# A three-stage decoder layer: running sums through memory in the mixer, TensorE's attention loop written out, GpSimd's order moved

## The chip, the core and the metric
One core of a Trainium2 chip runs the whole kernel. The time is device microseconds (us) of one execution; three runs of the kernel before are shown, and one more execution carries the profile. TensorE (PE) multiplies into eight banks of PSUM, VectorE (DVE) and ScalarE (ACT) work on PSUM and SBUF, GpSimd (POOL) on SBUF alone, SyncE (SP) issues most DMAs.

## The reference
The input x has 32 sequences of 128 tokens with 128 features. Cut to what matters:

```python
# 1. mixer: 4 heads of 64, state 128, the first 32 features of B and C rotated
alpha = exp(A_t * dt_t); gamma = tr * dt; beta = (1 - tr) * dt * alpha
base = b_t * (x_{t-1} * beta + x_t * gamma)
state = state * alpha + rotated(base, theta_t);  y_t = <state, rotated(c_t)>
x = layernorm(x + ((y + D * x_h) * silu(z)) @ w_out.T)
# 2. cross attention: 16 heads of 8 on ctx_1024, masked softmax over 128 keys
x = layernorm(x + softmax(mask(q @ k.T / sqrt(8))) @ v @ Wo + bo)
# 3. 16 experts of 64, top 2 of 4 groups, top 4 experts, and a shared expert
x = layernorm(x + (x + experts(x) + shared(x)))
```

## The kernel before, in words
The sequences go in eight groups of four, b = 0 to 3. There are three stages, each a block of five engine programs written by hand and tied by semaphores; between blocks all engines meet. `pairs` (line 85) and `ahead` (line 95) run the groups two to a loop turn: `pairs` three turns and two groups written out, `ahead` two turns and four groups written out. `left` is how many groups follow.

**Mixer.** The recurrence is computed as a product per sequence: mix(s, t) = G(s, t) times exp(sum of the exponents A*dt from s+1 to t), zero for s > t, and y = w_tok times mix, with w_tok = gamma * x_s + beta * x_(s-1). The exponents' sums are made per sequence: GpSimd multiplies an upper triangle by the exponent of each head, twice, for a high and a low part (`ramps`, lines 728 to 734), TensorE multiplies both by a strict lower triangle (`after`) and adds a mask of -30000 (`acausal`) into one bank, PD (`front`, line 854), and ScalarE takes one exponential of 4 x 128 columns (line 693). The other bank of `front`, PX, holds x of the tokens and of the tokens before them (`tokens`, line 865); VectorE scales its halves by gamma and beta (`inputs_of`, line 785). PG holds G (`scores`). `back` (line 897) makes y in PY0 and PY1, `skip` (line 888) starts them with D * x, once a group; its six products mark where a group begins on TensorE. Beside a group runs the preparation of the next: `theta` (cumulative angles), `angles`, `fractions` (VectorE, lines 383 to 391), `sines`, `features` (B and C, in P0 and P1), `rotate` (VectorE, lines 761 to 770), `gates`. VectorE forms x + output and its statistics, GpSimd normalises (`normalise_pool`, lines 141 to 148). In the last group the attention's first projections are mixed in: `part_third` is GpSimd's part of them, after which SP stores the parts (line 265) and loads them stacked (line 276, eight DMAs for the keys and eight for the queries).

**Attention.** In TensorE's group g (line 1473) run the transposed scores and products of g, the scores of g+1 (VectorE reduces their maxima, line 1237, and splits them in three bf16 parts, `split_maxima`, lines 1248 to 1261; TensorE transposes the parts in `max_rows`, line 1457) and the projections of g+2 from x1, staged by SP in `xs` (line 1029), and from the context. GpSimd per group casts the masks (`masks`), makes the projections' third parts and the context's remainder (`context_lo`), normalises the group before and adds the output bias (`biased`, line 1081). In group 5 it issues the loads of the expert weights, in group 6 it splits them (`split_weights`, lines 1623 to 1626); at the head of group 7 TensorE, VectorE and ScalarE wait for that (`e.steps`, PREPARED).

**Experts.** Not touched.

## Time and profile before

| | us |
|---|---|
| median of 3 runs | 678.86 |
| lowest, highest | 673.94, 679.98 |
| the profiled execution | 679.41 |
| its span, first to last instruction | 677.7 |
| TensorE busy (matmuls) | 600.6, 89% |
| VectorE busy | 498.2, 74% |
| GpSimd busy | 261.2, 39% |
| ScalarE busy | 255.8, 38% |

The mixer's preparation ends at some 46 us, its groups at 249, the attention at 473; the experts take the rest. A matmul's recorded end is modelled and overlaps the next one's start, so what a TensorE instruction takes is read from start to start. "issue" names time in which an engine waited for nothing that the profile shows. The mean granted TensorE clock is 0.96 of full speed.

### The profile page before, as it was taken

Reading aid. Unit: us, or ns where it says so; the run is one execution under the profiler, and the core shown is the slowest. Engines: PE = TensorE matmul, PEld = TensorE weight load, DVE = VectorE, ACT = ScalarE, POOL = GpSimd, SP = SyncE. Lnnn points to the kernel's source line nnn. Section 1 sums busy time; section 2 is a strip of 40 time slices with the busy share of each in tenths; the row PEclk is TensorE's granted clock in tenths of the full one; section 3 lists DMA queues with packets and bytes.
Section 4 is the critical chain, followed back from the end, with each engine's and each line's share of the span. In section 5 each row is a group of like instructions: output and inputs, shape, how many; then the busy total and the mean of one; then the engine's idle time right before and its main releaser. Section 6 shows DMA issues by size and latency. Waiting matters only on the chain. (4 is left out here: it accounts for less than half of the span.)

```text
span 677.7 us, 17999 instructions
## 1 busy us (share of the span) xinstructions
PE 600.6 (89%) x6368; PEld 494.8 (73%) x6368; DVE 498.2 (74%) x1246; ACT 255.8 (38%) x444; POOL 261.2 (39%) x301
## 2 busy tenths in 40 slices
PE   6589999999999855699799999877999999999994
PEld 6467777777787643578678777655888888888884
DVE  3867977977977738368688888656688787887863
ACT  2443533533543320356446655343332232232220
POOL 4264646647645628624244346091110110110111
PEclk9979999999999978699899999899999999999998
DMA  7020000000000067064464555400000000000000
GB/s 211 0 63 1 17 15 0 15 15 0 15 16 1 12 176 219 17 171 138 124 176 117 142 133 154 119 7 2 32 1 32 31 0 32 31 29 2 17 16 16
DMA packets 39186, 39.29 MB, mean 58 GB/s; under 512 B 4609, under 2 KB 30753, under 8 KB 39121
## 3 DMA queue, kind: packets, MB, share of 16 engines
q1 hardware_dynamic: 37200, 35.69, 18.4%
q0 software_dynamic: 704, 1.92, 1.1%
q10 hardware_dynamic: 1216, 0.79, 0.5%
q8 instruction: 44, 0.72, 0.5%
q14 instruction: 22, 0.17, 0.1%
HBM read 24.10 MB, written 10.88 MB: 52 GB/s over the span
## 5 line engine op out<-in xcount | busy, mean ns | idle before, releaser
L1911 PE MATMUL bank<-xT_hl_c,w_up 128*128 128x512 f32 x432 | 119.7, 413 | 2.4 <-ACTq L67 2.4
L141 POOL TENSOR_TENSOR rstd<-mv,norm_c 128x4 f32<-128x4 f32 x24 | 6.4, 268 | 272.0 <-DVE mv L135 257.1
L1237 DVE TENSOR_REDUCE nmax<-bank 128x4 f32<-128x512 f32 x112 | 72.0, 685 | 31.0 <-PE bank L1393 26.7
L1145 ACT ACTIVATE prob<-bank 128x512 f32<-128x512 f32 x128 | 69.4, 594 | 56.1 <-PE bank L1393 46.8
L1911 PEld LDWEIGHTS bank<-xT_hl_c,w_up 128*128 128x128 f32 x432 | 77.2, 192 | 16.2 <-ACTq L67 2.6
L1833 ACT ACTIVATE sg<-bank 128x512 f32<-128x512 f32 x72 | 43.0, 597 | 106.7 <-PE bank L1911 106.7
L1927 PEld LDWEIGHTS bank<-w_down,hid 128*128 128x128 f32 x576 | 74.4, 191 | 5.9 <-issue 0.5
L732 POOL TENSOR_TENSOR ramp<-upto,dec_hl 128x512 fp32r<-128x512 f32 x64 | 66.8, 1072 | 27.2 <-PE bank L860 27.2
L1927 PE MATMUL bank<-w_down,hid 128*128 128x128 f32 x576 | 75.6, 275 | 0.0
L1383 PE MATMUL bank<-neg_i,mask 64*128 64x256 bf16 x512 | 52.7, 286 | 17.9 <-ACT prob L1145 5.8
L1866 DVE TENSOR_TENSOR gu<-sg,bank 128x512 f32<-128x512 f32 x64 | 43.9, 685 | 21.9 <-PE bank L1911 10.0
L1870 DVE TENSOR_TENSOR hid<-gu,bank 128x512 f32<-128x512 f32 x64 | 44.0, 688 | 7.1 <-DVE gu L1866 1.0
L868 PE MATMUL bank<-w_x,xhl 128*128 128x256 f32 x192 | 42.2, 329 | 0.0
L1383 PEld LDWEIGHTS bank<-neg_i,mask 64*128 64x128 bf16 x512 | 16.9, 97 | 33.2 <-issue 11.7
L1437 PE MATMUL bank<-prob,v_d 128*32 128x128 f32 x1024 | 36.4, 286 | 0.0
L1433 PE MATMUL bank<-prob,ones_s 128*32 128x128 f32 x1024 | 34.6, 276 | 0.8 <-ACT prob L1145 0.8
L420 PE MATMUL bank<-xhl,w_feat 128*128 128x512 f32 (+1 forms) x96 | 29.9, 447 | 5.4 <-DVE b_rot L766 4.4
L868 PEld LDWEIGHTS bank<-w_x,xhl 128*128 128x128 f32 x192 | 29.6, 191 | 6.1 <-issue 5.3
L880 PE MATMUL bank<-c_rot,b_rot 128*128 128x256 f32 x128 | 32.8, 378 | 0.0
L1433 PEld LDWEIGHTS bank<-prob,ones_s 128*32 128x32 f32 x1024 | 26.0, 109 | 6.1 <-issue 2.2
L1437 PEld LDWEIGHTS bank<-prob,v_d 128*32 128x32 f32 x1024 | 28.2, 114 | 2.9 <-ACT prob L1145 0.2
L1071 POOL CAST mask<-mask 128x512 bf16<-128x512 uint8 x32 | 19.3, 612 | 27.3 <-PE bank L1393 22.2
(227 smaller groups left out, 1250.1 us busy)
## 6 DMA issues: line engine op xcount, KB each, us to landing
k_stack<-k_scratch SPq DMA_DIRECT2D x32, 128.0 KB, 2.7
q_stack<-q_scratch SPq DMA_DIRECT2D x32, 128.0 KB, 2.9
k_scratch<-k_part SPq DMA_DIRECT2D x16, 192.0 KB, 2.5
q_scratch<-q_part SPq DMA_DIRECT2D x16, 192.0 KB, 2.5
x<-xT_in SPq DMA_DIRECT2D x8, 256.0 KB, 8.4
mask<-mask_in SPq DMA_DIRECT2D x8, 256.0 KB, 4.7
xres<-x_in SPq DMA_DIRECT2D x8, 256.0 KB, 2.9
k_stack<-k_scratch SPq DMA_DIRECT2D x32, 64.0 KB, 3.0
```

Source lines behind the costliest of these rows:

```text
L732: pool.tensor_tensor(ramp[:, b % 2, v, :, :], bc(upto[:, None, :], [P, HEADS, P]), bc(dec_hl[:, v, bass.ds(g * GS + b, 1), :].rearrange("p ...
L868: mm = pe.matmul(PX[:, shift * D_INNER:(shift + 1) * D_INNER], xhl[:, par, a, b, 1 - shift:P + 1 - shift], w_x[:, v, :], start=(n == 0), s ...
L1145: act.activation(prob[:, b % 2, ORDER[n], :, :], (TT0, TT1)[n % 2][:, :], ACT.Exp, scale=XD ** -0.5)\
L1237: dve.tensor_reduce(nmax[:, b, 4 * u:4 * u + 4], (SS0, SS1)[n % 2][:, :].rearrange("p (i k) -> p i k", i=4), AX_X, ALU.max, negate=True).t ...
L1383: pe.matmul(banks[j][:, :].rearrange("p (i h k) -> p i h k", i=4, h=2)[:, :, half, :], mask[rows, par, b, kind + ver, :], bc(neg_i[rows, N ...
L1433: mm = pe.matmul(U1[32 * u:32 * u + 32, 0:P], ones_s[:, 4 * b + i, :, :].rearrange("p r c -> p (r c)"), prob[:, b % 2, u, i, :], start=(b ...
L1437: mm = pe.matmul(U0[32 * u:32 * u + 32, b * P:(b + 1) * P], v_d[:, par, b, i * P + 32 * u:i * P + 32 * u + 32], prob[:, b % 2, u, i, :], s ...
L1833: act.activation(sg[:, k, :], GG[k][:, :], ACT.Silu).then_inc(a_s.sem, 1)
L1866: dve.tensor_tensor(dst, sg[:, k, :], UU[k][:, :], ALU.mult).then_inc(v_gu.sem, 1)
L1870: dve.tensor_tensor(hid[:, c, :], gu[:, k, :], WW[(c - 1) % 2][:, :], ALU.mult).then_inc(v_hid.sem, 1)
L1911: mm = pe.matmul(bank[:, :], w_up[:, which, a, c, :], xT_hl[par][:, v, :], start=(n == 0), stop=(n == 2))
L1927: mm = pe.matmul(PO[:, b * P:(b + 1) * P], hid[:, c, b * P:(b + 1) * P], w_down[:, c, :], start=(c == 0 and b == 0), stop=(c == NC - 1), s ...
```

## The change
Mixer: the sums of the exponents are formed once for half of the sequences at a time, by two products with the upper triangle: one gives them as rows (64 rows of sequence and head, 128 tokens), one as columns. ScalarE copies both out, the columns negated (`upto_s`); SP stores the rows in DRAM and loads each sequence's four rows back to all 128 partitions (`load_row`). GpSimd sets the acausal half to -30000 (`causal`), and ScalarE takes four exponentials, one a head, with the negated column as bias (`expos`), one sequence ahead. Ramps, the strict triangle and PD are gone; PX has two banks in turn. VectorE's operations on the two halves of fractions, rotation and inputs become one each. GpSimd's normalisation waits for the next fraction. Attention: TensorE's eight groups are written out, and it transposes x1 in place (`xs` and its DMA are gone); GpSimd's context remainder and last masks move ahead of the normalisation, which waits for the end of VectorE's split of the maxima.

The pieces are, in order: the sums and rows; fractions; GpSimd's mixer group; rotation; GpSimd's attention group; the end of TensorE's attention.

```diff
+        def sums(pe, half, bank):
+            dec = decay[:, HALVES[half], :].rearrange("p b h -> p (b h)")
+            pe.wait_ge(s_coef, half + 1)
+            pe.matmul(bank[64 * half:64 * half + 64, 0:P], dec, upto[:, :], start=True, stop=True)
+            pe.matmul(bank[:, P:P + 64], upto[:, :], dec, start=True, stop=True).then_inc(s_sums, 1)
+        def load_row(sp, g, b):
+            sp.wait_ge(s_exp.sem, s_exp.at(g - 1, HEADS * b + HEADS - 1))
+            sp.dma_start(rows[:, b, :, :], rows_dram[bass.ds((g * GS + b) * HEADS, HEADS), :]
+                         .rearrange("h t -> (h t)").partition_broadcast(P).rearrange("p (h t) -> p h t", h=HEADS))\
+                .then_inc(s_row[b].sem, 16)
+        def causal(pool, g, b):
+            pool.wait_ge(s_row[b].sem, s_row[b].at(g))
+            pool.affine_select(out=rows[:, b, :, :], in_=rows[:, b, :, :], compare_op=ALU.is_ge, fill=NEG, base=0,
+                               pattern=[[0, HEADS], [1, P]], channel_multiplier=-1).then_inc(s_sel.sem, 1)
+        def expos(act, g, b):
+            act.wait_ge(s_sel.sem, s_sel.at(g, b))
+            act.wait_ge(s_mix.sem, s_mix.at(g, b - 2))
+            for h in range(HEADS):
+                act.activation(expo[:, b % 2, h, :], rows[:, b, h, :], ACT.Exp,
+                               bias=upto_s[:, bass.ds(g * GS + b, 1), h]).then_inc(s_exp.sem, 1)
...
         def fractions(dve, g):
-            for k in range(2):
-                dve.wait_ge(s_ang.sem, s_ang.at(g, k))
-                dve.tensor_scalar(whole[:, k, :], ang[:, k, :], ROUND, -ROUND, ALU.add, ALU.add).then_inc(s_whole.sem, 1)
-            for k in range(2):
...
+            dve.wait_ge(s_ang.sem, s_ang.at(g, 1))
+            dve.tensor_scalar(whole[:, :, :], ang[:, :, :], ROUND, -ROUND, ALU.add, ALU.add).then_inc(s_whole.sem, 2)
+            dve.wait_ge(s_whole.sem, s_whole.at(g, 1))
+            dve.wait_ge(s_trig.sem, s_trig.at(g - 1, 1))
+            dve.tensor_tensor(frac[:, :, :], ang[:, :, :], whole[:, :, :], ALU.subtract).then_inc(s_frac.sem, 2)
...
             def group(g, par, left):
-                ramps(g, (2, 3))
-                if left:
-                    ramps(g + 1, (0, 1))
                 if left == 2:
                     steps_of(pool, g + 2)
                 if left:
+                    for b in range(GS):
+                        causal(pool, g + 1, b)
+                    if left == 2:
+                        pool.wait_ge(s_frac.sem, s_frac.at(g + 2, 1))
                     normalise_pool(pool, g, s_res, s_x1, res, mv, rstd, norm_c, x1[:, bass.ds(g * GS, GS), :])
...
             def rotate(g, par):
-                for k in range(2):
-                    dve.wait_ge(s_trig.sem, s_trig.at(g, k))
-                    dve.tensor_tensor(b_rot[:, par, k, :], P0[:, :], trig[:, k, :], ALU.mult).then_inc(s_prod.sem, 1)
+                dve.wait_ge(s_trig.sem, s_trig.at(g, 1))
+                dve.tensor_tensor(b_rot[:, par, :, :], bc(P0[:, None, :], [P, 2, GT]), trig[:, :, :], ALU.mult).then_inc(s_prod.sem, 2)
                 dve.wait_ge(s_feat.sem, s_feat.at(g, 1))
-                for k in range(2):
-                    dve.tensor_tensor(c_rot[0:64, par, k, 0, :], P1[0:64, :], trig[0:64, k, :], ALU.mult)
-                    dve.tensor_tensor(c_rot[64:P, par, k, 1, :], P1[64:P, :], trig[64:P, k, :], ALU.mult).then_inc(s_prod.sem, 1)
+                for j in range(2):
+                    half = slice(64 * j, 64 * j + 64)
+                    dve.tensor_tensor(c_rot[half, par, :, j, :], bc(P1[half, None, :], [64, 2, GT]), trig[half, :, :], ALU.mult)\
+                        .then_inc(s_prod.sem, 1)
...
-            def group(g, par, left):
-                if left >= 2:
-                    masks(g + 2, par, (2,))
+            def rest(g, par, left):
                 if left >= 3:
                     context_lo(g + 3, 1 - par)
                 if left >= 2:
-                    masks(g + 2, par, (3,))
+                    masks(g + 2, par, (2, 3))
+
+            def group(g, par, left):
                 if left == 2:
                     load_weights(pool, d, e)
                 if left == 1:
                     split_weights(pool, e)
                 if left:
                     head(g + 1, 1 - par, left - 1)
+                    rest(g + 1, 1 - par, left - 1)
+                    if left >= 2:
+                        pool.wait_ge(v_split.sem, v_split.at(g + 2, 7))
                     normalise_pool(pool, g, v_res, g_out, res, mv, rstd, norm_c, x2[:, bass.ds(g * GS, GS), :])
                     biased(g + 1)
...
-            ahead(pe, group)
+            for g in range(NG):
+                group(g, g % 2, NG - 1 - g)
```

On TensorE in the mixer, one sequence of the loop's body before, from `front` on (waits in brackets):

```order
L859 MATMUL bank<-ramp,after 128x512 [waits expo_ready]
L859 MATMUL bank<-ramp,after 128x512
L860 MATMUL bank<-acausal,ident 128x512
L868 MATMUL bank<-w_x,xhl 128x256 [waits w_ready]
L868 MATMUL bank<-w_x,xhl 128x256 x2
L900 MATMUL bank<-mix,w_tok 64x128 [waits w_ready]
L900 MATMUL bank<-mix,w_tok 64x128 x3
L868 MATMUL bank<-w_x,xhl 128x256 x3
L877 MATMUL bank<-plain 128x512 [waits mix_ready]
```

The same in the change:

```order
L912 MATMUL bank<-w_x,xhl 128x256 [waits w_ready]
L912 MATMUL bank<-w_x,xhl 128x256 x5
L943 MATMUL bank<-mix,w_tok 64x128 [waits w_ready]
L943 MATMUL bank<-mix,w_tok 64x128 x3
L920 MATMUL bank<-plain 128x512 [waits mix_ready]
```

Three wide products are gone, and all six token products stand ahead of the back products.

On GpSimd at the end of the attention before, from the last load of the expert weights through group 5's normalisation and bias to the weights' split (max_parts is VectorE's split of the maxima):

```order
L1615 DMA bias<-gate_bias_in 128x16
L141 TENSOR_TENSOR rstd<-mv,norm_c 128x4 [waits x2_sum_ready]
L142 TENSOR_TENSOR res<-res,mv 128x512
L144 TENSOR_TENSOR rstd<-rstd,norm_c 128x4 [waits x2_ready]
L148 TENSOR_TENSOR x<-res,rstd 128x512 [waits x2_ready]
L1081 TENSOR_TENSOR xb<-x,b_o 128x512 [waits x2_sum_ready]
L1623 CAST w_up<-w_raw 128x1152 [waits expert_weights]
```

And in the change:

```order
L1657 DMA bias<-gate_bias_in 128x16
L141 TENSOR_TENSOR rstd<-mv,norm_c 128x4 [waits x2_sum_ready,max_parts]
L142 TENSOR_TENSOR res<-res,mv 128x512
L144 TENSOR_TENSOR rstd<-rstd,norm_c 128x4 [waits x2_ready]
L148 TENSOR_TENSOR x<-res,rstd 128x512 [waits x2_ready]
L1118 TENSOR_TENSOR xb<-x,b_o 128x512 [waits x2_sum_ready]
L1665 CAST w_up<-w_raw 128x1152 [waits expert_weights]
```

The normalisation of group 5 has one wait more, max_parts, and the weights' split is queued behind it.

## Rows read from the trace of the kernel before

**Rows 1.** Busy time by stretch: mixer, attention (us and instructions; granted clock, DMA share, GB/s).
```profile
46.00:222.00 176.00, 170.79 (x1062) 135.78 (x1061) 141.74 (x285) 72.16 (x105) 94.41 (x91) 1.00 0.03 9
276.00:473.00 197.00, 171.96 (x3738) 138.28 (x3737) 145.59 (x334) 99.60 (x189) 82.05 (x93) 0.97 0.40 112
```

**Rows 2.** Timeline of TensorE in one mixer group (start, us, line, xcount, [idle before]).
```profile
110.59 0.62 PE L859 MATMUL bank<-ramp,after 128*128 128x512 f32 x2
111.09 0.70 PE L868 MATMUL bank<-w_x,xhl 128*128 128x256 f32 x3
111.73 0.66 PE L900 MATMUL bank<-mix,w_tok 128*64 128x128 f32 x8
112.32 0.62 PE L868 MATMUL bank<-w_x,xhl 128*128 128x256 f32 x3
112.77 0.86 PE L877 MATMUL bank<-plain 96*128 96x512 f32 x3
114.15 1.76 PE L420 MATMUL bank<-xhl,w_z 128*128 128x512 f32 x6
```

**Rows 3.** Timeline of TensorE: first and last start of the skip product, of eight.
```profile
47.58 1.66 PE L893 MATMUL bank<-xhl,w_dx 128*128 128x512 f32 x6
222.33 1.65 PE L893 MATMUL bank<-xhl,w_dx 128*128 128x512 f32 x6
```

**Rows 4.** Waits in the mixer: who for whom, us in total, times, longest.
```profile
PE bank L859 <- POOL ramp L732: 4.2, 6, 1.0
```

**Rows 5.** VectorE: line 391 of all groups (ns min/median/max); timeline of rounding and rotation.
```profile
L391 DVE TENSOR_TENSOR frac<-ang,whole x16: 676/680/1524, 31.0 to 202.6; 128x512 f32<-128x512 f32 x16
100.28 0.75 DVE L387 TENSOR_SCALAR whole<-ang 128x512 f32<-128x512 f32 x2
104.81 1.28 DVE L766 TENSOR_TENSOR b_rot<-bank,trig 128x512 f32<-128x512 f32 x2
```

**Rows 6.** Timeline of ScalarE: 128 elements, the exponential of 512, a table load.
```profile
17.08 0.31 ACT L552 ACTIVATE e<-soft 128x128 f32<-128x128 f32 x1 [2.13 <-DVE soft L603]
99.75 0.60 ACT L693 ACTIVATE expo<-bank 128x512 f32<-128x512 f32 x1 [1.43 <-PE bank L860]
101.73 1.28 ACT L368 ACT_TABLE_LOAD   x1 [1.38 <-DVE frac L391]
```

**Rows 7.** Timeline of GpSimd: an affine select of 512 elements.
```profile
264.19 0.88 POOL L1120 TENSOR_SCALAR_AFFINE_SELECT ones_s<-ones_s 128x512 f32<-128x512 f32 x1
```

**Rows 8.** DMA issues of the page (KB each, median us to landing).
```profile
xres<-x_in SPq DMA_DIRECT2D x8, 256.0 KB, 2.9
```

**Rows 9.** Timeline of TensorE, GpSimd and SP at the mixer's end.
```profile
232.48 0.72 PE L859 MATMUL bank<-ramp,after 128*128 128x512 f32 x2 [2.92 <-POOL ramp L732]
...
230.39 4.04 POOL L732 TENSOR_TENSOR ramp<-upto,dec_hl 128x512 fp32r<-128x512 f32 x4
...
244.50 4.02 SPq L276 DMA_DIRECT2D q_stack<-q_scratch  x8
```

**Rows 10.** Waits of TensorE in the attention.
```profile
PE bank L1457 <- DVE npart L1261: 6.1, 6, 1.7
```

**Rows 11.** VectorE: line 1257, one of the split's small operations (ns min/median/max).
```profile
L1257 DVE TENSOR_TENSOR nrest<-nmax,npart x16: 192/193/1248, 262.7 to 443.7; 128x32 f32<-128x32 f32 x16
```

**Rows 12.** Timeline of TensorE at the turn of the attention's loop.
```profile
332.34 0.39 PE L1383 MATMUL bank<-neg_i,mask 64*128 64x256 bf16 x4 [2.49 <-issue]
```

**Rows 13.** Timeline of TensorE in a group of straight code.
```profile
421.96 0.39 PE L1383 MATMUL bank<-neg_i,mask 64*128 64x256 bf16 x4 [0.84 <-issue]
```

**Rows 14.** Timeline of TensorE, GpSimd and VectorE around the last attention group.
```profile
432.70 0.61 PE L1383 MATMUL bank<-neg_i,mask 64*128 64x256 bf16 x4 [2.90 <-DMA q_stack<-max_scratch]
452.39 0.66 PE L1735 MATMUL bank<-ident,x 128*128 128x128 f32 x4 [1.10 <-POOL w_up L1626]
...
440.17 0.20 POOL L141 TENSOR_TENSOR rstd<-mv,norm_c 128x4 f32<-128x4 f32 x1 [15.34 <-DVE mv L135]
...
443.29 0.35 DVE L1255 CAST npart<-nmax 128x32 bf16<-128x32 f32 x1
```

More of the change, by code:

```diff
@@ L339, in mixer @@
         s_prod = sem("feat_dve", 8)
-        s_ramp = sem("ramp_ready", 8)
-        s_dec = sem("decay_mm", GS)
+        s_row = [sem(f"row_loaded{b}", 1, 16) for b in range(GS)]
+        s_sel = sem("row_causal", GS)
+        s_sums, s_summed = (ctx.enter_context(nc.semaphore(n)) for n in ("sums_mm", "sums_copied"))
+        s_stored = ctx.enter_context(nc.semaphore("rows_stored"))
+        pool_passed = ctx.enter_context(nc.semaphore("mixer_pool_passed"))
+        rows_dram = nc.dram_tensor("sum_rows_scratch", (NSEQ * HEADS, P), F32, kind="Internal").ap()
+        rows = sb("rows", [P, GS, HEADS, P])
         s_xx = sem("x_mm", GS)
         s_g = sem("g_mm", GS)
-        s_exp = sem("expo_ready", GS)
-        s_w = sem("w_ready", 3 * GS)
+        s_exp = sem("expo_ready", GS * HEADS)
+        s_w = sem("w_ready", 2 * GS)
         s_mix = sem("mix_ready", GS)
@@ L485, in _ @@
                 sp.dma_start(a.cin[:, :, :], d["ctxT"][:, 0:2 * GT].rearrange("p (g t) -> p g t", t=GT)).then_inc(s_att, 16)
+                for b in range(GS):
+                    s_row[b].prime(sp)
+                store_sums(sp, 0)
+                sp.wait_ge(s_stored, 16)
+                for b in range(GS):
+                    load_row(sp, 0, b)
+                store_sums(sp, 1)
                 sp.wait_ge(s_att, 9 * 16)
@@ L489, in _ @@
             def _(pool):
-                for s in (s_ramp, s_turns):
+                for s in (s_sel, s_turns):
                     s.prime(pool)
@@ L533, in _ @@
                 pe.wait_ge(s_pool, 2)
+                sums(pe, 0, PX0)
                 theta(pe, 0)
@@ L536, in _ @@
                 features(pe, 0, 0, (0, 1))
+                sums(pe, 1, PX1)
             @block.scalar
@@ L655, in group @@
                     .then_inc(s_x.sem[par], 16)
+                if left:
+                    for b in range(GS):
+                        load_row(sp, g + 1, b)
                 if not left:
@@ L726, in _ @@
                 s.prime(pool)
-            def ramps(g, bs):
-                for b in bs:
-                    pool.wait_ge(s_dec.sem, s_dec.at(g, b - 2))
-                    for v in range(2):
-                        pool.tensor_tensor(ramp[:, b % 2, v, :, :], bc(upto[:, None, :], [P, HEADS, P]),
-                                           bc(dec_hl[:, v, bass.ds(g * GS + b, 1), :].rearrange("p o h -> p (o h)")[:, :, None],
-                                              [P, HEADS, P]), ALU.mult).then_inc(s_ramp.sem, 1)
             def group(g, par, left):
-                ramps(g, (2, 3))
-                if left:
-                    ramps(g + 1, (0, 1))
                 if left == 2:
@@ L742, in group @@
                 if left:
+                    for b in range(GS):
+                        causal(pool, g + 1, b)
+                    if left == 2:
+                        pool.wait_ge(s_frac.sem, s_frac.at(g + 2, 1))
                     normalise_pool(pool, g, s_res, s_x1, res, mv, rstd, norm_c, x1[:, bass.ds(g * GS, GS), :])
@@ L747, in group @@
                 if left == 1:
-                    pool.memset(a.first[1][:, :, :, :].bitcast(F32), TWO_ONES).then_inc(a.ones, 1)
+                    pool.memset(a.first[1][:, :, :].bitcast(F32), TWO_ONES).then_inc(a.ones, 1)
+            for b in range(2):
+                causal(pool, 0, b)
             coefficients(pool, 1)
-            ramps(0, (0, 1))
             betas(pool, 1)
             steps_of(pool, 1)
+            for b in range(2, GS):
+                causal(pool, 0, b)
             pairs(pool, group)
```

140 lines of the change are left out of this document (66 added, 74 removed).

## The prediction

> **What bounds the kernel now.** I read the stretches of busy time first, then TensorE's own line in each, then its waits, and only then the engines it waits for. In the mixer (46 to 222 us) and in the attention (276 to 473 us) TensorE is the busiest engine, 171 us of 176 and 172 of 197, with VectorE next at 142 and 146 [rows 1]. The busy share alone doesn't say that TensorE is the bound, so look at one sequence of the mixer: its pieces stand back to back [rows 2]. The third stage, the experts, is untouched by the change and keeps its time. The chain of waits on the page covers only that stage, so it says nothing of the two that change, and I leave it.
>
> **The mixer's steady part.** Between the first and the last start of the skip product lie 222.33 - 47.58 = 174.8 us, seven groups [rows 3]. What the change takes from TensorE is, per sequence, the two ramp products and the mask product. Their starts take 111.09 - 110.59 = 0.50 us; the mask product's own run falls under the next record: the three token products behind it take 111.73 - 111.09 = 0.64 us, the same three without it 112.77 - 112.32 = 0.45 us [rows 2]. So 0.50 + 0.19 = 0.69 us a sequence, 28 sequences between the two marks: 19.3 us. TensorE's waits on the ramps between the marks, 4.2 us in all [rows 4], go too.
>
> What comes next late? VectorE's rotation. Before, the sine of the first half could start when the first fraction was done; now one fraction operation covers both halves, the sines wait for it, and one operation waits for both sines. From the end of the first mix: rounding and fraction about 2.0 us (two roundings take 0.75 us, two fractions 2 x 0.68 less the overlap), the table load 1.28 us, two sines of about 0.6 us each, and rotation in three operations of 1,024 elements, about 1.2 us each by the pair at 1.28 [rows 5, 6]: 8.1 us. TensorE meanwhile has back products 0.59, scores 1.38, features 1.6, six token products 0.90, back 0.59, scores 1.38 and half of features 0.8 [rows 2]: 7.2 us, and then wants the rotated C. I therefore charge a new wait of 0.6 us a group (it can be nothing, and 1.5 if VectorE is held up): 7 x 0.6 = 4.2 us back. Nine VectorE operations fewer a group save a start each, under 0.1 us, and a fraction that collides with GpSimd runs up to 1.52 us instead of 0.68 [rows 5]; the normalisation now starts behind it. I take nothing for that by itself: it is what lets VectorE keep pace with a shorter group. Sum: 19.3 + 4.2 - 4.2 = 19.3, taken as **19 us**. Bounds: 10 (VectorE doesn't keep pace: a new wait of 1.9 us a group) and 26 (no new wait, and what TensorE waits for a mix gone too).
>
> What is added is off this path. ScalarE runs four exponentials of 128 elements with a bias for one of 512: by the row of 128 elements 4 x 0.31, and no row has a bias from a tile at this size, so I allow 0.1 for it: 1.2 to 1.6 us against 0.60 [rows 6], four times a group, 4 us on an engine busy 72 us of 176 [rows 1]; each is done one sequence ahead of its mix. Were that cover gone, each sequence would pay 0.6 to 1.0 us. GpSimd's causal select takes 0.88 us by the nearest row of its size [rows 7] in place of two ramps; queued behind it are the next steps and the normalisation, which nobody wants for half a group. SP issues four loads of 256 KB a group; a load of that size lands in 2.9 us [rows 8], and at least a third of a group lies between a row's release and its use.
>
> **The mixer's start.** GpSimd's exponent product now stands ahead of the turns (+0.3 us), the merged fraction delays the first sine (+0.6), and the stage's first block ends only after ScalarE's two copies of the second sums and SP's store (+0.6). Against it, the first group's three products and the wait for the ramps go. Net +0.5, bounds 0 and +2.
>
> **The mixer's end.** In the last group TensorE waits 2.92 us for a ramp, and GpSimd's third part of the keys starts only behind four ramps, at 230.39 + 4.04 = 234.4; SP's sixteen loads of the stacks hang on it, and their last eight are issued until 244.50 + 4.02 = 248.5 us, which ends the stage [rows 9]. Without ramps that part starts when they did, at 230.4, 4.0 us earlier. The store, the landing and the stacks follow at the same distance. **-4.4 us** (the queries' part gains a little more), bounds -2 and -5.
>
> **The attention.** Three edits have a price.
> - Once a group, six times, TensorE waited for VectorE's split of the maxima, 6.1 us in all [rows 10]. Its small operations take 0.19 us, but up to 1.25 when GpSimd's biases and remainders run [rows 11]. GpSimd now waits for the end of that split. Of the 6.1 us I leave out the longest, 1.7, which I place before the last group, where a later wait covers it (below): -4.4 us, taken as -4.5.
> - TensorE's loop is written out. At the turn of the loop it stands 2.49 us with nothing to wait for [rows 12], and its clock then drops for a while; the same product takes 0.61 instead of 0.39 us after such a stop [rows 12, 14]. Half speed over some 3 to 4 us costs about 1.5 more, with a short stop behind it: -4.5 us. In written-out code it once stood 0.84 us for the same reason, while the weights were loading [rows 13]. The Trainium skill ("Runtime: NRT & Kernel Launch", section on instruction fetch mechanics) says that straight code is fetched ahead and mostly hidden; by the page nothing comes back, by that row up to 2.5 us over three new straight groups. I take nothing, and keep 2.5 in the range.
> - GpSimd's new wait stands ahead of group 5's normalisation, and behind it are the bias and the splitting of the expert weights, for which TensorE waits at the last group. Before, that chain began at 440.17 and TensorE went on at 452.39, 12.2 us later, after 1.10 us of waiting. Now it can't begin before the split of the last maxima ends: it starts at 443.29 and takes 4 x 0.19 us and its gaps, 444.1 [rows 11, 14]. TensorE then goes on at 456.3: **+4.0 us**, and as it stands there for 456.3 - (452.39 - 1.10 - 1.7) = 6.7 us, another 1.5 at half speed: +5.5. This is where the change costs.
> The weights' own loads are issued some 4 us later than before; the 2.90 us that TensorE waits for a row of maxima behind them [rows 14] may move either way: 0, bounds -3 and +3. The direct use of x1 instead of a staged copy removes a DMA that nobody waited for: 0. Sum of the attention: -4.5 - 4.5 + 5.5 = **-3.5 us**.
>
> **Total.** 679.4 (the profiled execution, 0.6 us above the runs' median) - 19 - 4.4 + 0.5 - 3.5 = 653.0, so 652.5 in terms of the median. I say 653.
>
> **Rivals.**
> - **VectorE becomes the mixer's bound.** Causal selects read and write SBUF too; if they hold up VectorE's operations on two SBUF tiles as other GpSimd work does (1.52 against 0.68 us [rows 5]), four a group of 0.88 us [rows 7] cost up to 3.5 us a group, and half of it on the path takes 12 us of the 19 back: 665. For it: VectorE is busy 142 of 176 us already. Against: the ramps were 64 such operations of 1.0 us [rows 9] and the path still was TensorE's. The page "SBUF — State Buffer" of the Trainium skill (section on who interferes with whom) gives this as a rule: a VectorE instruction with two SBUF inputs contends with a GpSimd one that reads SBUF, and one waits the other out. Chance 0.2.
> - **Row loads bound the mixer; slower than before.** Each load reads the same 2 KB for all 128 partitions; no row shows a broadcast of this size. Four a group must pass in the time of one group, about 25 us. At 2.9 us each [rows 8] they fit twice over; from 25 / 4 = 6.3 us a load on, the mixer is slower than today, and at 8 us it takes 32 us a group, 7 x 7 = 49 us more, less what the end still gains: 720. Chance 0.04.
> - **More than I count.** No new wait at the rotation, the others gone too, and no wait behind the weights: 26 + 4.4 + 6.5 = 37: 642. Chance 0.12.
> - **The attention loses.** The late chain takes the weights and the wait for maxima with it, stops of instruction fetch appear: +8 us: 661. Chance 0.09.
> My forecast, 647 to 659, gets 0.55.
>
> **Numbers.** About 1% (7 us) is what a measurement of this kernel can tell from no change. The range 642 to 667 holds the forecast, the third rival, the fourth and most of the first. Faster by over 1% (below 672): 0.90; within 1%: 0.05, the worst of the first and the fourth together; slower by over 1%: 0.05.
>
> **What to look at afterwards.** The starts of the skip product should lie 22.3 us apart on average, 25.0 before. The fraction should run in about 1.2 us, never over 2; the small operations of the split at 0.19 us without exception; no stop at the loop's turn; the stage's last stack issue some 23 us earlier than 248.5. In the last attention group TensorE should stand 6 to 7 us for the split weights, with the low clock behind it. I am wrong if TensorE waits for mix or for the rotation by over 1 us a group, if a load of a row takes over 6 us, or if the stop at the weights is short.

## The result

The changed kernel takes 655.6 us (median of 4 runs, 655.1 to 656.8) where the kernel before took 677.8 on the same chip (4 runs, 673.9 to 680.0): ratio 0.9669, 95% interval 0.9635 to 0.9703. The forecast was 653, the range 642 to 667. The profiled execution took 656.8, its span is 655.0. Run again later beside the last experiments it gave 655.8 us, ratio 0.9653 (0.9616 to 0.969).

### The profile page after: what moved, and what is told of

The parts are those of the page before. It is cut to its first block and busy times, and to the rows that moved or that the text cites. A ratio compares the mean times of both kernels' runs of the same rounds, so it can differ in the third digit from the quotient of the medians.

```text
span 655.0 us, 17900 instructions
## 1 busy us (share of the span) xinstructions
PE 582.7 (89%) x6280; PEld 484.8 (74%) x6280; DVE 474.6 (72%) x1174; ACT 277.4 (42%) x544; POOL 208.0 (32%) x260
## 3 DMA queue, kind: packets, MB, share of 16 engines
q1 hardware_dynamic: 41104, 42.57, 22.4%
## 5 line engine op out<-in xcount | busy, mean ns | idle before, releaser
L1953 PE MATMUL bank<-xT_hl_c,w_up 128*128 128x512 f32 x432 | 118.1, 409 | 2.4 <-ACTq L67 2.4
L141 POOL TENSOR_TENSOR rstd<-mv,norm_c 128x4 f32<-128x4 f32 x24 | 4.8, 201 | 299.9 <-DVE mv L135 178.7
L1424 PE MATMUL bank<-neg_i,mask 64*128 64x256 bf16 x512 | 52.8, 286 | 14.1 <-ACT prob L1186 5.7
L477 ACT ACTIVATE expo<-rows,neg_sums 128x128 f32<-128x128 f32 x128 | 40.9, 391 | 13.5 <-DVE mix L858 13.4
L422 PE MATMUL bank<-xhl,w_feat 128*128 128x512 f32 (+1 forms) x96 | 32.2, 461 | 9.0 <-DVE b_rot L817 4.5
L1424 PEld LDWEIGHTS bank<-neg_i,mask 64*128 64x128 bf16 x512 | 16.9, 97 | 29.8 <-ACT prob L1186 11.2
L920 PE MATMUL bank<-plain 96*128 96x512 f32 x96 | 30.8, 429 | 0.0
L912 PEld LDWEIGHTS bank<-w_x,xhl 128*128 128x128 f32 x192 | 27.8, 193 | 3.3
L422 PEld LDWEIGHTS bank<-xhl,w_feat 128*128 128x128 f32 (+1 forms) x96 | 17.3, 190 | 17.1 <-DVE c_rot L821 8.5
L1478 PEld LDWEIGHTS bank<-prob,v_d 128*32 128x32 f32 x1024 | 27.8, 113 | 2.9 <-issue 0.2
```

The lines of the kernel that those rows point to most:

```text
L422: mm = pe.matmul(bank[0:m, :], w[:, i, :], xhl[:, par, v, :, 1:], start=(n == 0), stop=(n == 2))
L477: act.activation(expo[:, b % 2, h, :], rows[:, b, h, :], ACT.Exp, bias=upto_s[:, bass.ds(g * GS + b, 1), h]).then_inc(s_exp.sem, 1)
L1424: pe.matmul(banks[j][:, :].rearrange("p (i h k) -> p i h k", i=4, h=2)[:, :, half, :], mask[rows, par, b, kind + ver, :], bc(neg_i[rows, N ...
L1478: mm = pe.matmul(U0[32 * u:32 * u + 32, b * P:(b + 1) * P], v_d[:, par, b, i * P + 32 * u:i * P + 32 * u + 32], prob[:, b % 2, u, i, :], s ...
L1953: mm = pe.matmul(bank[:, :], w_up[:, which, a, c, :], xT_hl[par][:, v, :], start=(n == 0), stop=(n == 2))
```

## The profile after the change

Line numbers of the changed kernel are higher: the skip product is L936 (893 before), token products L912 (868), back product L943 (900), features L422 (420), mix L858 (806), rotation L817 and L821 (766, 770), the first attention product L1424 (1383), the transposes behind the weights' wait L1777 (1735), the product that makes the attention's values L1392 (1351), called the value product below. A mark is the start of such an instruction, found in both traces.

Busy time by stretch of the changed kernel (us and instructions of each engine, then granted clock, DMA share, GB/s); the first and third row answer to [rows 1]:
```profile
46.00:207.00 161.00, 153.57 (x982) 125.12 (x981) 132.81 (x223) 92.35 (x194) 50.36 (x64) 1.00 0.20 58
232.00:257.00 25.00, 16.38 (x157) 13.46 (x158) 17.95 (x44) 2.02 (x4) 17.81 (x23) 0.64 0.48 129
257.00:454.00 197.00, 174.56 (x3749) 140.44 (x3749) 131.91 (x335) 100.38 (x191) 85.68 (x100) 0.95 0.38 106
```
VectorE is busy 82% of the mixer's stretch now, TensorE 95% (81% and 97% before). The second row is the attention's start; the same 25 us of the kernel before read:
```profile
251.00:276.00 25.00, 15.73 (x163) 12.60 (x163) 16.74 (x44) 2.02 (x4) 19.53 (x25) 0.71 0.55 151
```

The first and last skip product of TensorE, answering to [rows 3], and the first product of the attention's start:
```profile
48.99 1.65 PE L936 MATMUL bank<-xhl,w_dx 128*128 128x512 f32 x6
...
207.54 1.65 PE L936 MATMUL bank<-xhl,w_dx 128*128 128x512 f32 x6
...
232.27 3.76 PE L285 MATMUL bank<-w_out,y 128*128 128x128 f32 x16 [6.64 <-issue]
```
Seven groups take 158.55 us instead of 174.75: 22.65 a group. Putting the marks side by side gives the whole difference of the two traces:

| stretch | before | after | change |
|---|---|---|---|
| up to the first skip product | 47.58 | 48.99 | +1.4 |
| seven groups of the mixer | 174.75 | 158.55 | -16.2 |
| last skip product to the attention's first product (L285) | 28.77 | 24.73 | -4.0 |
| from there to the value product (L1392) of the first group in the steady part | 46.04 | 48.80 | +2.8 |
| five groups, value product to value product | 119.87 | 114.76 | -5.1 |
| last of them to the transposes behind the weights (L1777) | 35.38 | 35.22 | -0.2 |
| to the start of the last products | 213.94 | 212.66 | -1.3 |
| sum | | | -22.6 |

TensorE's waits between the first and the last skip product, before and then after (who for whom, us, times, longest):
```profile
PE bank L859 <- POOL ramp L732: 4.2, 6, 1.0
PE bank L900 <- DVE mix L806: 1.0, 2, 0.5
```
```profile
PE bank L422 <- DVE c_rot L821: 3.7, 6, 0.7
PE bank L943 <- DVE mix L858: 3.6, 8, 0.5
```
So TensorE's own work between the marks fell from 174.75 - 5.2 = 169.55 to 158.55 - 7.3 = 151.25, by 18.3 us or 0.65 us a sequence, and waits of 7.3 us stand where 5.2 stood. One group in TensorE's timeline, and VectorE's beside it:
```profile
97.37 0.66 PE L943 MATMUL bank<-mix,w_tok 128*64 128x128 f32 x8 [0.42 <-DVE mix L858]
...
105.61 0.95 PE L422 MATMUL bank<-xhl,w_feat 128*96 128x512 f32 x3 [0.66 <-DVE c_rot L821]
106.40 0.87 PE L912 MATMUL bank<-w_x,xhl 128*128 128x256 f32 x6
107.82 0.66 PE L943 MATMUL bank<-mix,w_tok 128*64 128x128 f32 x8 [0.55 <-DVE mix L858]
```
```profile
93.10 0.43 DVE L847 TENSOR_TENSOR w_tok<-xg 128x256 f32<-128x256 f32 x1
93.44 0.68 DVE L124 SCALAR_TENSOR_TENSOR res<-xres,bank 128x512 f32<-128x512 f32 x1
94.16 0.87 DVE L131 BATCH_NORM_STATS2 stats<-res 128x6 f32<-128x128 f32 x4
95.19 0.38 DVE L135 BATCH_NORM_AGGREGATE mv<-stats 128x2 f32<-128x6 f32 x4 [0.16 <-DVE stats L131]
95.95 0.69 DVE L397 TENSOR_TENSOR xhl<-x,xhl 128x512 fp32r<-128x512 f32 x1 [0.39 <-issue]
96.56 0.68 DVE L858 TENSOR_TENSOR mix<-bank,expo 128x512 f32<-128x512 f32 x1
97.16 0.68 DVE L390 TENSOR_SCALAR whole<-ang 128x1024 f32<-128x1024 f32 x1
98.04 1.23 DVE L393 TENSOR_TENSOR frac<-ang,whole 128x1024 f32<-128x1024 f32 x1 [0.20 <-DVE whole L390]
...
99.99 0.93 DVE L847 TENSOR_TENSOR w_tok<-xg 128x256 f32<-128x256 f32 x1
...
101.95 1.22 DVE L817 TENSOR_TENSOR b_rot<-bank,trig 128x1024 f32<-128x1024 f32 x1 [0.43 <-ACT trig L372]
103.09 2.46 DVE L821 TENSOR_TENSOR c_rot<-bank,trig 64x1024 f32<-64x1024 f32 x2
...
106.32 0.77 DVE L847 TENSOR_TENSOR w_tok<-xg 128x256 f32<-128x256 f32 x1
```
VectorE has almost no gap from the residual at 93.44 to the third mix at 107.01: its chain is as long as TensorE's half group. The sum w_tok (L847, both inputs in SBUF) takes 0.42 us where GpSimd stands idle. Twice in this chain it takes longer, beside these two pieces of GpSimd's work, the normalisation and the causal selects:
```profile
99.60 1.04 POOL L142 TENSOR_TENSOR res<-res,mv 128x512 f32<-128x512 f32 x1
...
104.99 1.82 POOL L469 TENSOR_SCALAR_AFFINE_SELECT rows<-rows 128x512 f32<-128x512 f32 x3
```
That is 0.85 us of the chain in such a group. Over the seven groups the 27 sums between the marks take 16.7 us, 5.3 more than at 0.42 each; before, 28 took 16.0, 4.1 more.

The attention, TensorE's waits from 232 to 431 us and the product behind the weights; they answer to [rows 10, 13, 14]:
```profile
PE bank L1498 <- DVE npart L1302: 5.0, 2, 2.6
PE bank L1424 <- issue: 3.4, 3, 1.8
PE bank L1424 <- DMA q_stack<-max_scratch: 1.1, 1, 1.1
...
431.05 1.12 PE L1777 MATMUL bank<-ident,x 128*128 128x128 f32 x4 [6.93 <-POOL w_up L1668]
```
The two waits for the split parts (npart) are both in the attention's start (at 246 and 253 us); in the groups behind it there are none, where before there were six.

The stop of [rows 13], read again with the queue of SP beside it, before and then after:
```profile
416.73 3.01 SPq L276 DMA_DIRECT2D q_stack<-q_scratch  x4
...
DMA to landing us min/median/max: 2.5/3.0/8.2
```
```profile
304.62 1.70 SPq L276 DMA_DIRECT2D q_stack<-q_scratch  x4
...
310.02 0.39 PE L1424 MATMUL bank<-neg_i,mask 64*128 64x256 bf16 x4 [1.77 <-issue]
```
TensorE's stop of 0.84 us ended at 421.96, 2.2 us after the last issue of a query stack (416.73 + 3.01); a stack takes 2.5 to 8.2 us from issue to landing (the second row, over all DMAs into the query stacks). After the change the stops named "issue" stand at the same product of a group, the one that takes up the next group's stacks, 3.7 us behind their last issue. They are waits for the stacks: the last of the four loads was issued at 305.89 and took 4.04 us to land, at 309.93, and TensorE went on at 310.02. At the two other such stops, and at the one of the kernel before, the time between landing and going on is the same 0.1 us.

## The experiments

All ratios are to the kernel before, run on the same chip; the changed kernel stands at 0.9669 and 0.9653.

| kernel | us | ratio (95%) |
|---|---|---|
| changed mixer, attention of before | 664.4 | 0.9772 (0.9719 to 0.9826) |
| mixer of before, changed attention | 675.7 | 0.9961 (0.9939 to 0.9982) |
| loop and staging back | 663.3 | 0.9778 (0.9737 to 0.9819) |
| staging back alone | 656.1 | 0.962 (0.9556 to 0.9685) |
| no wait for the split | 651.4 | 0.9579 (0.9529 to 0.9629) |
| weights split first | 645.4 | 0.9491 (0.9433 to 0.9549) |
| rounding to rotation in halves | 653.8 | 0.9614 (0.9567 to 0.9661) |
| statistics behind the rotation | 666.9 | 0.979 (0.9735 to 0.9845) |
| changed kernel again | 655.8 | 0.9653 (0.9616 to 0.969) |
| statistics in VectorE's gap | 652.6 | 0.9608 (0.957 to 0.9646) |
| three edits combined | 644.9 | 0.9514 (0.9471 to 0.9557) |
| all four | 646.1 | 0.9522 (0.9489 to 0.9555) |

### The two halves of the change, each alone

The function of the mixer from one kernel, that of the attention from the other.

> The changed mixer with the attention of before. By the marks of the two traces the mixer's part of the change (start +1.4, seven groups -16.2, end -4.0) is worth -18.8 us, and the attention's -2.5. Theory (the stages add up): 677.8 - 18.8 = 659.0, range 657 to 661, and TensorE's wait for the split weights back to about 1 us. Rival A (the attention edits are worth what was predicted or more, 5 us): 661 or above in sum with a run of the attention alone at 672 or below. Rival B (the stages do not add: the new mixer alone already brings all): 655 to 656.5.

> The mixer of before with the changed attention. Theory: 677.8 - 3.8 (attention -2.5 and the 1.3 us that the experts' stage shows less after it) = 674.0, range 673 to 676, and the start of the attention as in before (46.0 us from the out product to the first value product, 48.8 in the changed kernel), which would make it nearer 672. Rival A (the attention edits lose what they win): 677 to 679. Rival B (as predicted, -3.5): 674.3; the two are not told apart by the time but by the terms: wait on the weights, waits on the split of the maxima, stops without a reason.

The mixer alone is worth 2.3% or 15.5 us, the attention alone 0.4% or 2.6 us, both together 22.4. The attention's small worth is as the marks say. The mixer's was 3.3 us less than the marks of the changed kernel, although they repeat in its own trace (158.5 us over seven groups). What is missing is lost in the attention of before behind the faster mixer: 209.2 us from its first product to the transposes, 201.3 in the kernel before. The group with the turn of the loop is 2.5 us longer, and its stop is:
```profile
318.62 0.61 PE L1426 MATMUL bank<-neg_i,mask 64*128 64x256 bf16 x4 [4.41 <-issue]
```
It was 2.49 us in [rows 12]. More lies in the attention's start (+1.6) and in its first group (+2.9, in it a wait of 1.5 us for the stacks). At 664.4 us the kernel fits none of the three expectations of its run (the one from 661 us on asked for the attention alone at 672 or below): the stages don't add up exactly, and the price of a loop's turn isn't a constant. The attention alone, 675.7 us, lies in its range.

### Loop and staging

TensorE's loop and the staged copy back (the second kernel: the staging only, the groups written out):
```diff
-            for g in range(NG):
-                group(g, g % 2, NG - 1 - g)
+            ahead(pe, group)
+                sp.dma_start(xs[:, par, :, :], x1[:, bass.ds(g * GS, GS), :]).then_inc(d_xs.sem[par], 16)
...
-                transpose_x1(pe, a, t, x1[:, g * GS:(g + 1) * GS, :], PO)
+                transpose_x1(pe, a, t, xs[:, par], PO)
```

> The changed kernel with TensorE's attention again as a loop over two groups, twice, and x1 staged by a DMA again as the loop needs. My prediction's term (the loop's turn costs a 2.49 us stop and 1.5 us of low clock, straight code nothing): 655.6 + 4.5 = 660. Theory after the trace of the changed kernel (its straight code stands 3.4 us in three stops without a reason, the kernel before 3.3 us in two: the stop is moved, not removed, and only the low clock behind it is saved): 656 to 657.5. Rival (the stops in the straight code are the larger cost): 654 or below.

> The changed kernel with TensorE's attention still written out, but x1 staged by SP's DMA of 256 KB a group again, and read from the staged copy. My prediction (nobody waited for the staging: 0): 655.6. Theory from the run with loop and staging back together (663.3, of which the turn of the loop shows 3.8 us between two value products and the four other intervals 3.2 us more): the staging delays the stacks of keys and queries that TensorE takes up once a group, 658.8, with waits on the stacks of 4 to 6 us in sum instead of 3.4. Rival (the rest of the loss is the loop too): 655 to 656.

The staging costs nothing that can be measured (0.962 against 0.9653, intervals overlapping), as predicted; my theory of 3.2 us for it fell. With the loop too the time is 663.3 us, above all that was expected (660 at most). The loop costs 663.3 - 656.1 = 7.1 us, and by the marks 205.6 against 198.4 us from the attention's first product to the transposes. The group with the turn is 28.1 us long instead of 23.6 with the staging alone: 4.5 us, the size of my term. Its stop:
```profile
317.02 0.40 PE L1430 MATMUL bank<-neg_i,mask 64*128 64x256 bf16 x4 [2.78 <-issue]
```
The two kernels ran on different chips, so the marks count here. The other 2.7 us are spread over the groups before and behind it (0.7 in the first, and longer waits for stacks behind); why they come with the loop isn't settled. The reading "the stop is moved into straight code, not removed" also fell: the stops of straight code are there with the loop and without. With the loop the profile itself names the DMA of the query stacks as what four of them waited for (1.32, 1.17, 0.36 and 1.14 us). What the Trainium skill says ("Runtime: NRT & Kernel Launch", instruction fetch mechanics), that straight code is fetched ahead and that a taken branch can stall on its target's page, agrees with both: a stop of 2.5 to 4.4 us at the turn, none of its own in straight code. That the stop at the turn is one of instruction fetch is not shown by any run; the trace gives no reason for it.

### GpSimd's wait for the split

```diff
                     if left >= 2:
-                        pool.wait_ge(v_split.sem, v_split.at(g + 2, 7))
```

> The changed kernel without GpSimd's wait for the end of VectorE's split of the maxima, in every group. My prediction's terms: the waits for the split come back (+4.5), the chain to the expert weights starts 4 us earlier (-5.5): 654.6. Theory A (both terms right): 654 to 655.5, with waits of 4 to 6 us in all on the split and a wait on the weights under 4 us. Theory B (the contention is moved by the new order of masks and remainders already, so the wait brings nothing): 650 to 652. Theory C (the split's delays cost more than the weights' wait): 657 to 659.

651.4, 4.4 us less than the changed kernel and 3 less than my own terms give. The end of the last attention groups in its trace:
```profile
420.42 0.27 PE L1496 MATMUL bank<-ident,npart 128*48 128x128 bf16 x2 [1.71 <-DVE npart L1300]
...
425.58 0.66 PE L1775 MATMUL bank<-ident,x 128*128 128x128 f32 x4 [1.10 <-POOL w_up L1666]
```
The wait on the weights is 1.10 again, as in [rows 14], and one wait for the split is back, at the last group (1.71 us), where it was 1.65 before. In the five groups ahead of it there is none, though nothing holds GpSimd off now: the wait isn't what took those away. Before, the split ran beside GpSimd's bias, masks and remainder, and its operations of 0.19 us took up to 1.24; now these five splits run beside the power of four columns (L144) at 0.18 to 0.22 us. That is what the new order of masks and remainders would do; TensorE's written-out code is in this kernel too, and no run has it with the old order. The wait that I credited with 4.5 us saves 1.7 us once and costs 5.8.

### The weights split ahead of the wait

```diff
-                if left == 1:
-                    split_weights(pool, e)
...
+                    if left == 2:
+                        split_weights(pool, e)
                     if left >= 2:
                         pool.wait_ge(v_split.sem, v_split.at(g + 2, 7))
```

> The changed kernel with the splitting of the expert weights ahead of GpSimd's wait in group 5, right behind the loads, instead of behind the bias of group 6. Theory (the 6.9 us that TensorE stands for the split weights is the late chain alone, and 1 to 1.5 us of low clock hang on it): 655.6 - 7 = 648.5, range 647 to 650, and no wait on the weights. Rival A (GpSimd's 7.4 us of splitting from about 412 us then collides with VectorE's split of the maxima at 418 and TensorE waits there by 1 to 2 us more, as in the kernel before): 650 to 651.5, no better than the run without the wait. Rival B (what is gained there is lost at the next wait, a row of maxima): 653 or above.

645.4 us: 10.4 below the changed kernel, 7.5 of it by the marks from the last value product to the transposes (27.8 against 35.2 us), which now follow without a wait. Another 1.7 lie ahead of the first skip product, which the edit doesn't touch, and the rest isn't told from what two chips differ by. The expected time was 647 to 650. GpSimd, VectorE and TensorE there:
```profile
409.92 5.24 POOL L1668 TENSOR_TENSOR w_up<-w_raw,w_up 128x1152 fp32r<-128x1152 f32 x2
```
```profile
413.87 1.33 DVE L1296 CAST npart<-nmax 128x32 bf16<-128x32 f32 x1
```
```profile
416.01 0.27 PE L1498 MATMUL bank<-ident,npart 128*48 128x128 bf16 x2 [0.19 <-DVE npart L1302]
```
The collision that rival A expected is there: the cast of 0.18 us took 1.33, until GpSimd's subtraction ended at 415.2. It hit one operation only and TensorE waited 0.19 us. The Trainium skill ("SBUF — State Buffer", who interferes with whom) names casts too among the VectorE operations that can contend with GpSimd, and says that the one issued second is blocked; this row agrees. In the changed kernel GpSimd had stood idle at that place for 12 us:
```profile
418.90 0.20 POOL L141 TENSOR_TENSOR rstd<-mv,norm_c 128x4 f32<-128x4 f32 x1 [12.31 <-DVE npart L1302]
```
So the late chain was a matter of order, not of capacity.

### Who makes TensorE wait in the mixer

First the halves back, as the kernel before had them:
```diff
-            dve.tensor_scalar(whole[:, :, :], ang[:, :, :], ROUND, -ROUND, ALU.add, ALU.add).then_inc(s_whole.sem, 2)
+            for k in range(2):
+                dve.wait_ge(s_ang.sem, s_ang.at(g, k))
+                dve.tensor_scalar(whole[:, k, :], ang[:, k, :], ROUND, -ROUND, ALU.add, ALU.add).then_inc(s_whole.sem, 1)
```
(fraction, and both rotations, alike; that makes ten VectorE operations of five, not the nine of the expectation). Then the residual's statistics out of VectorE's chain, in two places:
```diff
-                    residual_dve(dve, g, PO, xres[par][:, :, :], s_x1, s_res, dve_passed, res, stats, mv)
+                    residual_sum(dve, g, PO, xres[par][:, :, :], s_x1, s_res, res)
...
+                if stats_of is not None:
+                    statistics(dve, stats_of, s_res, dve_passed, res, stats, mv)
```

> The changed kernel with rounding, fraction and rotation in two halves again, as in the kernel before (nine VectorE operations for five). My prediction's theory (the merged fraction makes the sines late, and TensorE waits 0.6 us a group for the rotation because of it): 655.6 - 3.7 = 652, rotation waits gone. Theory V (VectorE is busy without a gap from the residual to the third mix of each group; the waits of TensorE for mix and rotation are that chain's, not the sine's; more operations make it 0.1 to 0.3 us longer a group): 655.5 to 658, rotation and mix waits between the first and last skip product 7 us as before or more.

> The changed kernel with VectorE's statistics of the residual (0.87 + 0.16 + 0.38 = 1.41 us a group) moved behind the next group's rotation. Theory V (VectorE's chain from the residual to the third mix sets the first half of the group; TensorE waits 7.3 us in it between the first and last skip product): 1.41 us off that chain, 7 times, less what TensorE itself then binds: -6 us, 649.6, range 648 to 651, and skip products 21.8 us apart instead of 22.65. Rival A (the waits come from the sine's way, ScalarE and table load, which the statistics do not touch): -1 to -2. Rival B (the normalisation now runs beside the rotation's neighbours and slows them): 655 or above.

> The changed kernel with the statistics of the residual (1.41 us a group) moved behind the next group's third mix and its plain parts, where VectorE has 0.5 us free and TensorE's wait for the fourth mix has 1.2 us of slack, and with GpSimd's turns and causal selects ahead of the normalisation in its queue (the run before put the statistics ahead of the third mix, inside the same chain, and behind it GpSimd's normalisation held the selects up). Theory V (VectorE's chain from the residual to the third mix is what TensorE waits for, 7.3 us between the first and last skip product): waits fall to 1 to 3 us, skip products 21.9 to 22.1 us apart, total 5 us below the changed kernel. Rival (other waits take their place: GpSimd's normalisation now beside the token sums, or the wait for the fourth mix): within 2 us of the changed kernel.

Waits between the first and last skip product, of the halves and of the statistics in the gap (the changed kernel had 3.7 and 3.6):
```profile
PE bank L945 <- DVE mix L860: 3.9, 8, 0.7
PE bank L424 <- DVE c_rot L824: 2.3, 7, 0.4
```
```profile
PE bank L422 <- DVE c_rot L828: 3.2, 6, 0.6
PE bank L962 <- DVE mix L873: 1.0, 5, 0.2
```
The halves came out between the two theories: they shorten the wait for the rotation by 1.4 us and leave the mix, seven groups in 157.5 us instead of 158.5. That is 1.1 us of the 3.7 that my theory of the late sine gave; the total's difference (0.9614 against 0.9653) is not told from none. The statistics in the gap take 2.6 us off the waits for the mix: 156.0 us, and 652.6 against 655.8 in all. That is less than theory V asked for: 22.3 us a group for 21.9 to 22.1, and 3.2 us in all for 5. So the waits for the mix are VectorE's chain, as theory V says, and those for the rotation come in part from the sine's way. This kernel also has GpSimd's new order, and no run has that alone. It can't have made an exponential come in time, since VectorE waited for none between the marks of the changed kernel; but it moved the collisions too (27 sums w_tok in 15.1 us for 16.7), so how much of the 2.6 us belongs to the statistics isn't separated.

The first attempt with the statistics was 11 us slower (expected: 6 faster), and shows what else hangs there. Its seven groups take 164.8 us, 6.2 more, and 6.0 more follow behind the last skip product, where TensorE waits 7.95 us for one mix. TensorE, ScalarE and GpSimd in one group of it:
```profile
108.61 0.66 PE L953 MATMUL bank<-mix,w_tok 128*64 128x128 f32 x8 [2.06 <-DVE mix L864]
```
```profile
112.98 1.29 ACT L477 ACTIVATE expo<-rows,neg_sums 128x128 f32<-128x128 f32 x4 [6.50 <-POOL rows L469]
```
```profile
106.25 0.20 POOL L141 TENSOR_TENSOR rstd<-mv,norm_c 128x4 f32<-128x4 f32 x1 [16.82 <-DVE mv L135]
...
112.14 2.40 POOL L469 TENSOR_SCALAR_AFFINE_SELECT rows<-rows 128x512 f32<-128x512 f32 x4
```
Behind the rotation the statistics still stand ahead of the third mix, the last link of the chain: a bad place, by my mistake. And GpSimd's queue runs in order: its normalisation came 6 us later in the group (at 106.25 with the skip product at 95.27, for 99.45 with 94.59), and the turns and causal selects behind it held ScalarE's exponentials up by 6.5 us. That breaks the cover that my prediction gave the exponentials (one sequence ahead). In the kernel with the statistics in the gap GpSimd's turns and selects were put ahead of the normalisation.

### The changed kernel again, and what is best

> The changed kernel itself, run beside the two that follow, so that small differences can be read against it. Both theories: the ratio of the first measurement again, 0.967 of the kernel before (0.9635 to 0.9703); the runs with one edit taken back so far lay at 0.962 (staging back) and 0.9614 (unmerged), and whether these are gains of 3 us or the spread between chips is what this run tells.

> The changed kernel with three edits: the expert weights split ahead of GpSimd's wait (as in the run with the weights first), rounding, fraction and rotation in two halves again, and a wait that keeps GpSimd's last normalisation of the mixer off VectorE's first split of the maxima (where an operation of 0.19 us took 0.95 and TensorE waited 2.6 us). Expected from the parts: weights first -9 (0.9491 against 0.9669 of the kernel before is 12, the spread between chips taken off), unmerged -1.1 by the distance of the skip products, the start of the attention -1.3 to -2: 11.5 to 14 us below the changed kernel, 642 to 644. Rival (the parts do not add, as the mixer-only run showed with 5 us more than its mixer's gain explains): 645 to 648.

> The combined kernel (weights first, rounding to rotation in halves, the wait ahead of the mixer's last normalisation) with the statistics in VectorE's gap too. By the last runs the two edits of the mixer take different waits: the statistics the ones for the mix (3.5 to 1.0 us between the first and last skip product), the halves the ones for the rotation (3.7 to 2.3 us). Theory (with the chain shorter by 1.41 us the sines come earlier too, and both waits go): skip products 22.0 us apart, 154 us over seven groups against 157.5, total 3 us below the combined kernel, ratio 0.947 of the kernel before, 641 to 643. Rival (what TensorE doesn't wait for there it waits for at the next place): 0.951 to 0.953.

The repeat gave 0.9653, so 0.962 and 0.9614 are within the spread between chips. The combination has the weights first, the halves, and ahead of the mixer's last normalisation this wait:
```diff
+            pool.wait_ge(v_split.sem, v_split.at(0, 3))
             normalise_pool(pool, NG - 1, t["x1_res"], x1_out, res, mv, rstd, norm_c, x1[:, NSEQ - GS:, :])
```
Its 644.9 us are 10.9 below the repeat on the same chip, just short of the 11.5 to 14 expected, and it is no better than the weights first alone (0.9491), and the fourth edit added nothing (0.9522, the rival's figure, for 0.947; its seven groups take 157.5 us, as with the halves alone, against 156.0 with the statistics alone; why the two don't add isn't settled). With that wait the attention's start takes 47.5 us for 48.8: the first split of the maxima is undisturbed, and the second is hit instead (0.46, 0.53 and 0.52 us for operations of 0.19). That isn't shown to be the wait's gain, since the start took 47.6 and 47.7 us without it in the kernels with the weights first and with the statistics in the gap. The three kernels with the weights first beat both kernels by at least 1%: about 645 us, of which the one moved call for the weights brings nearly everything.

## Why the prediction was right, step by step

- **TensorE's products: right.** 0.65 us a sequence instead of 0.69: 18.3 for 19.3.
- **Waits in the mixer: the rotation right, the mix missed.** Ramp waits of 4.2 went; the rotation's came, 3.7 for 4.2 (my own chains, 8.1 against 7.2 us, gave 0.9 a group, and I charged 0.6 without saying why, so the closeness is in part luck). But "I take nothing for that by itself: it is what lets VectorE keep pace" was wrong: the waits for the mix grew from 1.0 to 3.6 us, VectorE being without a gap for half a group. This and the products make the 3 us between -16.2 and -19. The first rival had the right engine, and its mechanism is there, but small. The fraction ran in 1.22 us because the selects ran at other times. The one time they met, in the first group, it took 1.79 us and the select 1.62 instead of 0.64. The sums w_tok did meet them, 0.77 us for 0.42, and the normalisation, 0.93. All collisions of these sums come to 5.3 us over seven groups, about 1 more than before, and not to the 12 us of the rival.
- **Row loads: rival dead.** 256 KB land in 3.2 us, 5.8 at most, against the 6.3 us needed.
- **The mixer's start: +1.4 in this trace for +0.5**, but the same code began its first skip product at 47.3 to 48.6 us in six other traces. Not told from nothing.
- **The mixer's end: right**, -4.0 for -4.4; the last stack issue ended at 229.7, 18.8 us earlier.
- **The attention: the sum near (-2.5 for -3.5), two terms wrong.** The loop: 4.5 us at its turn, as charged, but 7.1 in all when it was put back. That term was 2.6 us too small, and why is open. The split: its waits in the groups went (4.5 us), but waits for the stacks grew from 1.6 to 3.4 us: what was next late, and I had named nothing, since I read one of those (0.84 us) as a stop of instruction fetch. The gain didn't come from the wait that I credited with it: without the wait it stayed. The late chain: 6.9 us for the 6.7 that I gave, with TensorE 5.8 us later. The clock was low behind it as said (0.51 of full speed in the 4 us from 431). The row of maxima went from 2.90 to 1.11, inside its bounds. So that the sum came near is in part luck: gains that I hadn't counted (1.8 us at the row of maxima, more at the loop) made up for a loss that I hadn't seen, the next one.
- **Not foreseen: +2.8 us in the attention's start.** GpSimd's last normalisation of the mixer now meets the first split (one operation at 0.95, one at 0.79 us, so "without exception" failed), and the 25 us from there ran at a granted clock of 0.64 instead of 0.71. The time goes with the operations of that split that are held up: with none the attention's start took 46.0 and 45.6 us (before, and the changed attention behind the old mixer), with one 47.6 to 47.7 in three kernels, with two or three 48.6 to 49.0 in seven. It does not go with the clock: at the same 0.705 four kernels took 45.6, 47.3, 47.6 and 49.0. No edit of the attention made it: the new mixer with the attention of before shows one such operation and 47.7 us. With the new mixer GpSimd begins that normalisation 9.4 us behind the first product for 9.7 before, and VectorE the split 11.1 to 11.7 us behind it for 11.4: shifts of 0.3 us, and they meet.

In sum -26.4 was forecast and -22.6 came: 2.8 us less in the mixer's groups, 0.9 at its start, 0.4 at its end and 1.0 in the attention, and 1.3 more behind it.

## What to carry to other kernels

When a stage loses work on its busiest engine, add up the second engine's chain between the same two marks before taking the whole gain: here TensorE waited 7.3 us for it over seven groups, 1.0 us a group. When a wait and a new order come in one edit, price them apart: without the wait the collisions of the groups stayed away, and the wait cost 5.8 us through a queue behind it. An unexplained stop that recurs at the same instruction of each group is first to be laid beside the DMA issues that this instruction needs.

## What the runs showed of the hardware

The turn of TensorE's loop cost a stop of 2.49, 2.78 and 4.41 us in three kernels whose loop is the same. A VectorE cast of 32 columns from SBUF took 1.33 us instead of 0.18 while one GpSimd operation of 2.6 us ran. A VectorE sum of 256 columns with both inputs in SBUF took 0.77 us beside a GpSimd select of 512 columns and 0.93 beside a subtraction of 512, for 0.42 alone, and beside GpSimd's power of four columns (1.02 us long) no small operation of the split took over 0.22. A DMA of 2 KB read for all 128 partitions (256 KB written) landed in 3.2 us, a plain load of that size in 3.7.
